# An expert's bias added by VectorE instead of by a product, and a residual sum moved from VectorE to GpSimd

## The chip, the core and the metric

The kernel runs on one core of one Trainium2 chip. Five engines work side by side, each through its own list of instructions in order: TensorE (PE, with its weight loads shown as PEld), VectorE (DVE), ScalarE (ACT), GpSimd (POOL) and SyncE (SP, which only issues transfers here). They meet through semaphores. The metric is the device time of one launch in microseconds (us). Before the change its median over three runs is 768.35 us (768.01 to 769.15).

## The reference

The input is 128 graphs of 128 nodes with 256 features. A graph layer comes first, then a layer of 16 experts with top-1 routing and a capacity of 1228 rows an expert.

```python
def gnn(X, A):                     # X: layer-normed x, A: adj, per graph
    Xw = X @ Wv + bv
    e = leaky_relu(sj[:, None, :] + si[:, :, None] + ab[0], 0.2)   # sj, si: Xw @ aw halves
    alpha = A * exp(e);  T = alpha / (alpha.sum(-1, keepdims=True) + 1e-12)
    H = 0;  Xk = X
    for k in range(3):
        H = H + Xk @ Wk[k] + bk[k];  Xk = T @ Xk
    return relu(H)

def experts(x):                    # x: all 16384 rows, layer-normed
    probs = softmax(x @ switch_w.T + switch_b);  route, p = argmax, max
    pos = rank of the row among those of its expert;  keep = pos < 1228
    y = x @ expert_w[route].T + expert_b[route]
    return where(keep, y, x) * p

x = x + gnn(layernorm(x), adj)
x = x + experts(layernorm(x))
```

## The kernel before

The graph layer goes graph by graph. One turn of the pipeline is called a slot here; slot `k` works on several graphs at once, each at another point of its way: graph `k` is multiplied with the weights, graph `k+2` is normalised by GpSimd (L475, `x`), and graph `k-2` (`LAG_X1`) gets its result. For that graph TensorE has summed the three products in PSUM (`ps_z0`), and VectorE adds the summed bias of the layer (L728, into `hb`), then does ReLU and the residual sum in one instruction (L739, `rows = max(hb, 0) + xin`). Mean and variance of the new row follow (L774, L798). TensorE transposes that row one slot later (L1188) for the logits (L1254); every fourth slot a group of four graphs is routed by some twenty small VectorE instructions. Ten slots behind its own (`LAG_OUT`) a graph's rows are scattered by GpSimd to a buffer in HBM, sorted by expert (L507, one indirect DMA for each graph).

From slot 32 on, as soon as enough rows of an expert are there, a slot also carries one tile of 128 rows of one expert. These 96 or so slots are called woven here; the tile is loaded by SP (L404), normalised by ScalarE (L646), transposed by TensorE (L1290), split in a rounded part (`xth`, ScalarE, L652) and a rest (`xtl`, VectorE, L1107, function `low`). TensorE then makes six products with the expert's weights and a seventh with its bias (L1311): `two_ones` (a matrix whose first two rows are ones) times `ebp` (the two parts of all 16 biases, in two partitions, all others zero). Which expert it is stands in a table (`tab_exp`), from which TensorE's sequencer loads a register (L1302). VectorE multiplies with the probability and adds the row (L1121, function `finish`), and GpSimd scatters the finished tile to the output (L524, a second indirect DMA in each woven slot). ScalarE also writes a default output for every graph (L588).

The tiles that are left when the graphs are through (46 of 143) run in a tail, `tile(i)` on each engine.

The order on each engine is written out by hand: `slot_fn(it, k)` of each engine's block lists what it does in a slot, `phase_a` calls it for all slots, and `woven(it, k)` and `tailed(it, k)` say which tile goes with it. GpSimd's list for a woven slot is: normalise (L475), scatter the tile (L524), scatter the row (L507), and in every fourth slot two powers and an update of the token numbers (L471, L485, L502). VectorE's list has `hb`, `finish`, `rows`, `xtl` of the next graph, the statistics, `svs` (a small operand that TensorE waits for, L783), `low`, and at the end the row softmax (`em`, `al`, `ri`, `tm`: L837, L846, L852, L857), whose `tm` TensorE transposes in the next slot (L1211).

## Time and profile before

| | |
|---|---|
| median of the runs | 768.35 us |
| the profiled execution | 767.28 us, its span 765.5 us |
| TensorE busy | 711.6 us (93%), granted clock 0.985 |
| VectorE busy | 647.9 us (85%) |
| ScalarE busy | 480.2 us (63%) |
| GpSimd busy | 444.1 us (58%) |

The span has four parts: a start up to about 26 us, 32 slots without a tile up to about 163 us, the woven slots up to about 664 us, and the last routing with the tail up to the end. A busy TensorE counts pipelined matmuls whose ends are modelled, so 100% does not by itself say that no faster pace is possible; it says that the engine was never seen waiting. Idle time of an engine that others do not wait for costs nothing.

### The profile page before, as it was taken

To read this page: it belongs to the slowest core of one execution; us is meant where nothing else is said; L and a number is where in the kernel's file an instruction comes from. 1 tells how busy PE (TensorE), PEld (TensorE's weight loads), DVE (VectorE), ACT (ScalarE), POOL (GpSimd) and SP (SyncE) were. 2 spreads that over 40 slices of the span, in tenths; PEclk is the share of its full clock that TensorE was granted. 3 is DMA by queue.
4 is the path that set the end of the run, shared out by engine and by line. 5 is a ranking of instruction groups with operands and counts; after the bars stand their busy time and mean duration, and the time that the engine had idled before them with its cause. 6 is when DMAs were issued, how large, how long until landed. Compare 5 with 4: busy or idle time off the path is not lost.

```text
span 765.5 us, 18802 instructions
## 1 busy us (share of the span) xinstructions
PE 711.6 (93%) x4791; PEld 624.2 (82%) x4791; DVE 647.9 (85%) x3100; ACT 480.2 (63%) x1504; POOL 444.1 (58%) x523
## 2 busy tenths in 40 slices
PE   1899999999999999999999999999999999877783
PEld 1788888778888888898889899898889899756663
DVE  3799999999989999899989999999989988785552
ACT  1457777766666666666666666666666766654551
POOL 4224445546666666666656666666666665575563
PEclk9999999999999999999999999999999999979998
DMA  9423444433344444444443344444443323353430
GB/s 266 118 85 97 138 138 154 151 127 119 123 144 153 147 146 153 128 150 139 146 141 118 121 143 149 145 140 147 134 134 128 115 89 101 99 167 112 120 104 1
DMA packets 93035, 100.15 MB, mean 131 GB/s; under 512 B 10427, under 2 KB 85240, under 8 KB 92930
## 3 DMA queue, kind: packets, MB, share of 16 engines
q1 hardware_dynamic: 77860, 66.74, 30.1%
q0 software_dynamic: 13008, 30.07, 10.8%
q10 hardware_dynamic: 2064, 2.13, 1.1%
q8 instruction: 44, 0.72, 0.4%
q14 instruction: 59, 0.48, 0.2%
HBM read 49.92 MB, written 54.72 MB: 137 GB/s over the span
## 4 chain that ended last, share of the span: by engine, by line
PE 86%; DVE 6%; issue 3%; ACT 1%; SPq 1%; DMA 1%; POOL 1%; POOLq 0%; DVEq 0%; ACTq 0%
PE ps_z12a L1160 11%; PE ps_z12b L1160 11%; PE ps_lgb L1160 9%; PE ps_z0a L1160 9%; PE ps_z0b L1160 8%; PE ps_lga L1254 6%; PE ps_z0b L1261 4%; PE ps_z0a L1261 4%; PE ps_z12b L1220 4%; PE ps_xt L1194 3%; PE ps_xt L1188 3%; PE ps_z12a L1220 3%; PE ps_lgb L1290 3%; PE ps_t L1242 2%; PE ps_t L1211 2%
## 5 line engine op out<-in xcount | busy, mean ns | idle before, releaser
L524 POOL DMA_INDIRECT out<-lent,tok x143 | 145.8, 1020 | 151.3 <-DVE lent L1121 136.0
L507 POOL DMA_INDIRECT rowbuf<-rows,idx x128 | 129.8, 1014 | 55.0 <-issue 30.1
L572 ACT CAST xth<-ps_xt 128x256 fp32r<-128x256 f32 x128 | 47.8, 373 | 123.6 <-PE ps_xt L1194 123.3
L475 POOL TENSOR_SCALAR x<-xin,nm,r 128x256 f32<-128x256 f32 x128 | 85.1, 665 | 27.6 <-PE ps_xt L1194 19.3
L1254 PEld LDWEIGHTS ps_lga<-swc,xft 128*128 128x128 f32 x512 | 76.8, 191 | 14.2 <-ACT xft L575 3.4
L646 ACT ACTIVATE x<-rin 128x256 f32<-128x256 f32 x143 | 86.8, 608 | 1.7 <-DMA rin<-rowbuf 1.7
L471 POOL TENSOR_TENSOR r<-ve,mhalf 128x4 f32<-128x4 f32 x32 | 34.2, 1069 | 77.7 <-ACT ve L618 77.7
L588 ACT ACTIVATE od<-rows,oc,oa 128x256 f32<-128x256 f32 x128 | 77.0, 602 | 0.1
L753 DVE TENSOR_TENSOR xtl<-ps_xt,xth 128x256 fp32r<-128x256 f32 x128 | 54.0, 422 | 20.6 <-ACT xft L575 19.6
L1254 PE MATMUL ps_lga<-swc,xft 128*128 128x16 f32 x512 | 66.2, 243 | 2.9 <-ACT xft L575 2.9
L1194 PE MATMUL ps_xt<-ident,x 128*128 128x128 f32 x256 | 49.5, 275 | 9.4 <-POOL x L475 8.5
L1160 PE MATMUL ps_z12b<-w12l,xth 128*128 128x512 f32 x128 | 57.7, 451 | 0.0
L1160 PE MATMUL ps_z12a<-w12l,xth 128*128 128x512 f32 x128 | 57.2, 447 | 0.0
L739 DVE SCALAR_TENSOR_TENSOR rows<-hb,xin 128x256 f32<-128x256 f32 x128 | 54.8, 429 | 1.5
L1160 PE MATMUL ps_lgb<-ewh,xth 128*128 x194 | 55.4, 367 | 0.5 <-issue 0.5
L817 DVE BATCH_NORM_STATS2 st<-xin 128x6 f32<-128x256 f32 x128 | 53.1, 415 | 1.5 <-DMA xin<-in_x 1.5
L1107 DVE TENSOR_TENSOR xtl<-ps_lgb,xth 128x256 fp32r<-128x256 f32 x112 | 46.8, 418 | 7.5 <-ACT xth L652 3.1
L774 DVE BATCH_NORM_STATS2 st<-rows 128x6 f32<-128x256 f32 x128 | 52.9, 413 | 0.0
L601 ACT ACTIVATE e<-ps_t,svs 128x128 f32<-128x128 f32 x128 | 47.1, 368 | 9.0 <-PE ps_t L1242 5.9
L652 ACT CAST xth<-ps_lgb 128x256 fp32r<-128x256 f32 x112 | 42.3, 378 | 15.6 <-PE ps_lgb L1290 15.5
L837 DVE TENSOR_TENSOR em<-e 128x128 f32<-128x128 f32 x128 | 38.3, 299 | 15.0 <-ACT e L602 12.0
L575 ACT COPY xft<-ps_xt 128x256 f32<-128x256 f32 x128 | 48.4, 378 | 3.8 <-PE ps_xt L1188 3.8
(205 smaller groups left out, 2358.8 us busy)
## 6 DMA issues: line engine op xcount, KB each, us to landing
rin<-rowbuf SPq DMA_DIRECT2D x143, 130.0 KB, 2.3
xin<-in_x SPq DMA_DIRECT2D x32, 512.0 KB, 4.0
out<-od SPq DMA_DIRECT2D x32, 512.0 KB, 5.4
ain<-in_adj SPq DMA_DIRECT2D x32, 256.0 KB, 4.6
ewr<-in_ewT SPq DMA_DIRECT2D x16, 256.0 KB, 2.9
out<-lent,tok POOLq DMA_INDIRECT x143, 3.0
rowbuf<-rin ACTq DMA_DIRECT2D x1, 2080.0 KB, 10.8
rowbuf<-rows,idx POOLq DMA_INDIRECT x128
```

The source lines that it names most:

```text
L475: pool.tensor_scalar(x0[:, g % 2, :], xin[:, g % BODY, :], nm1[:, q, g % G:g % G + 1], r1[:, q, g % G:g % G + 1], ALU.add, ALU.mult).then_ ...
L507: pool.indirect_dma_start(out=rowbuf, out_offset=bass.IndirectOffsetOnAxis(ap=idx[:, i:i + 1], axis=0), in_=rows[:, r, :], in_offset=None, ...
L524: pool.indirect_dma_start(out=out.rearrange("g n d -> (g n) d"), out_offset=bass.IndirectOffsetOnAxis(ap=tok[:, i % RY:i % RY + 1], axis=0 ...
L588: act.activation(od[:, b2 * G + j, :], rows[:, go % BODY, 0:D], ACT.Identity, bias=oc[:, b2, j:j + 1], scale=oa[:, b2, j:j + 1]).then_inc( ...
L646: act.activation(x0[:, xr(i), :], rin[:, i % RI, 0:D], ACT.Identity, bias=rin[:, i % RI, NMR:NMR + 1], scale=rin[:, i % RI, RSTD:RSTD + 1] ...
L739: dve.scalar_tensor_tensor(rows[:, r, 0:D], hb[:, g % 2, :], 0.0, xin[:, r, :], ALU.max, ALU.add).then_inc(s_x1, 1)
L753: dve.tensor_tensor(xtl[:, g % 2, :], ps_xt[:, 0:D], xth[:, g % 2, :].bitcast(F32), ALU.subtract).then_inc(s_x0l, 1)
L1160: return pe.matmul(psum_out, lhs_l if part == 2 else lhs_h, rhs_l if part == 1 else rhs_h, start=start, stop=stop, skip_group_check=True)
L1194: mm = pe.transpose(ps_xt[:, t * P:(t + 1) * P], x0[:, g % 2, t * P:(t + 1) * P], ident[:])
L1220: pe.matmul(ps_z12[d][:, D:2 * D], tt[:, d, :], z2[:, d, :], start=False, stop=True, skip_group_check=True).then_inc(s_tz2, 1)
L1254: mm = pe.matmul(ps_log[:, (b2 * G + j) * E:(b2 * G + j + 1) * E], xft[:, t * P:(t + 1) * P], swc[:, t, :], start=(t == 0), stop=(t == KT ...
L1261: pe.matmul(ps_z0[d][:, 0:D], tt[:, d, :], z1[:, d, :], start=False, stop=True, skip_group_check=True).then_inc(s_tz1, 1)
```

## The change

An expert's bias is no longer multiplied. All 16 biases (4096 numbers) are loaded once to every partition (`ebf`). In `low(i)`, right behind the rest part, VectorE adds bias times probability to the loaded row, in place; `finish(i)` is as before. VectorE therefore needs the expert's number as a register: it loads four at a time for the tiles of the woven slots and up to 16 at a time for the last 31. The product on TensorE, `two_ones`, the split of the biases and their way through HBM go.

The residual sum is rewritten: `relu(z + b) + x` is `max(z, -b) + (x + b)`. VectorE makes `hb = max(z, -b)` with `below = -b`; GpSimd makes `xb = x + b` ahead, and `rows = hb + xb`. Both additions stand in GpSimd's slot between the normalisation and the scatters. VectorE's statistics of the new row move from the middle of its slot to behind `low`.

```diff
@@ sync
-            sp.dma_start(ebr[:], eb).then_inc(d_eb, 16)
...
-            sp.wait_ge(s_eb, 2)
-            sp.dma_start(parts[0].bitcast(F32), ebh[:].bitcast(F32)).then_inc(d_ebp, 16)
-            sp.dma_start(parts[1].bitcast(F32), ebl[:].bitcast(F32)).then_inc(d_ebp, 16)
-            sp.wait_ge(d_ebp, 32)
-            sp.wait_ge(s_ebz, 1)
-            sp.dma_start(ebp[0:2, :].bitcast(F32), parts.rearrange("r e d -> r (e d)").bitcast(F32)).then_inc(d_ebp, 16)
+            sp.dma_start(ebf[:], eb.rearrange("(a e) d -> a (e d)", a=1).to_broadcast([P, E * D])).then_inc(d_eb, 16)
@@ gpsimd
-            pool.memset(two_ones[:].bitcast(F32), 0.0).then_inc(s_pc, 1)
...
+                g = k - LAG_X1
+                if valid(it, g):
+                    residual(it, g)
+                g = k - LAG_X1 + 1
+                if valid(it, g):
+                    biased_input(it, g)
                 i = woven(it, k - 1)
                 if i is not None:
                     scatter(i)
...
+            def biased_input(it, g):
...
+                ge(pool, s_x1, it * BODY + g - 1)
+                alone(pool)
+                pool.tensor_tensor(xb[:, g % 2, :], xin[:, g % BODY, :], bias[:], ALU.add).then_inc(s_xb, 1)
+
+            def residual(it, g):
...
+                pool.wait_ge(s_hb, it * BODY + g + 1)
+                pool.wait_ge(s_xb, it * BODY + g + 1)
+                alone(pool)
+                pool.tensor_tensor(rows[:, r, 0:D], hb[:, g % 2, :], xb[:, g % 2, :], ALU.add).then_inc(s_x1, 1)
...
-            pool.memset(ebp[:].bitcast(F32), 0.0).then_inc(s_ebz, 1)
@@ vector, slot_fn
-                    dve.tensor_tensor(hb[:, g % 2, :], ps_z0[g % 2][:, 0:D], bias[:], ALU.add).then_inc(s_hb, 1)
+                    dve.tensor_tensor(hb[:, g % 2, :], ps_z0[g % 2][:, 0:D], below[:], ALU.max).then_inc(s_hb, 1)
...
-                    dve.scalar_tensor_tensor(rows[:, r, 0:D], hb[:, g % 2, :], 0.0, xin[:, r, :], ALU.max,
-                                             ALU.add).then_inc(s_x1, 1)
...
-                    dve.bn_stats(st2[:, g % 2, :], rows[:, g % BODY, 0:D]).then_inc(s_st2, 1)
...
+                g = k - LAG_X1
+                if valid(it, g):
+                    dve.wait_ge(s_x1, n(g))
+                    dve.bn_stats(st2[:, g % 2, :], rows[:, g % BODY, 0:D]).then_inc(s_st2, 1)
@@ vector, tiles
+            def experts_of(i):
...
+                if i < STEPPED and i % G == 0 or i >= STEPPED and (i - STEPPED) % LOADED == 0:
+                    dve.wait_ge(s_tab, step_of(i))
+                    m = G if i < STEPPED else min(LOADED, NT - i)
+                    _, at_i = nc.values_load_multi_w_load_instructions(
+                        tab_exp[0:1, i:i + m], [mybir.EngineType.DVE], min_val=0, max_val=E - 1)
...
             def low(i):
...
+                experts_of(i)
+                own = rin[:, i % RI, :]
+                dve.scalar_tensor_tensor(own[:, 0:D], ebf[:, bass.ds(at.pop(i) * D, D)], own[:, PROB:PROB + 1],
+                                         own[:, 0:D], ALU.mult, ALU.add).then_inc(b_row, 1)
@@ tensor
-                pe.matmul(y, two_ones[:], ebp[:, bass.ds(e * D, D)], start=False, stop=True,
-                          skip_group_check=True).then_inc(b_y, 1)
+                mm.then_inc(b_y, 1)
```

The first place where the order moves is GpSimd's list in the woven slots. These rows of before cover one slot with the powers of the fourth slot and the one behind it; `x` is the normalised graph, `out<-lent` the scatter of a tile, `rowbuf<-rows` that of a row.

```order
L471 TENSOR_TENSOR r<-ve,mhalf 128x4 [waits s_ve1]
L475 TENSOR_SCALAR x<-xin,nm,r 128x256 [waits s_r1,s_x0t]
L524 DMA out<-lent,tok 16384x256 [waits b_fin]
L485 TENSOR_TENSOR rows<-ve,mhalf 128x4 [waits s_ve2]
L502 TENSOR_SCALAR rows<-rows 128x4 [waits s_slot,s_tok]
L507 DMA rowbuf<-rows,idx 21696x260 [waits s_tok]
L475 TENSOR_SCALAR x<-xin,nm,r 128x256 [waits s_x0t]
L524 DMA out<-lent,tok 16384x256 [waits b_fin]
```

The same place in the changed kernel:

```order
L461 TENSOR_TENSOR r<-ve,mhalf 128x4 [waits s_ve1]
L465 TENSOR_SCALAR x<-xin,nm,r 128x256 [waits s_r1,s_x0t]
L527 TENSOR_TENSOR rows<-hb,xb 128x256 [waits s_xb,s_hb,d_scat2,s_odw]
L517 TENSOR_TENSOR xb<-xin,bias 128x256 [waits s_x1]
L537 DMA out<-lent,tok 16384x256 [waits b_fin]
L481 TENSOR_TENSOR rows<-ve,mhalf 128x4 [waits s_ve2]
L498 TENSOR_SCALAR rows<-rows 128x4 [waits s_slot,s_tok]
L503 DMA rowbuf<-rows,idx 21696x260 [waits s_tok]
L465 TENSOR_SCALAR x<-xin,nm,r 128x256 [waits s_x0t]
L527 TENSOR_TENSOR rows<-hb,xb 128x256 [waits s_hb,s_xb]
```

Two additions of 128x256 stand between the normalisation and the first scatter in every slot, and the first of them waits for VectorE's `hb`.

The second place is the second half of VectorE's list in a woven slot, from `low` to the `tm` that TensorE waits for. Before:

```order
L817 BN_STATS st<-xin 128x6
L1107 TENSOR_TENSOR xtl<-ps_lgb,xth 128x256 [waits b_hi]
L837 TENSOR_TENSOR em<-e 128x128 [waits s_e]
L937 TENSOR_TENSOR pos<-ps_t,pos 128x80 [waits s_pos,s_pre]
L846 ISA al,rs<-ain,em 128x128 [waits d_a3,s_em]
L846 ISA rs 128x1
L946 TENSOR_TENSOR sel<-oh,pos 128x64 [waits s_oh,s_pos]
L852 RECIPROCAL ri<-rs 128x1 [waits s_al]
L950 TENSOR_REDUCE slot<-sel 128x4 [waits s_ro]
L857 TENSOR_SCALAR tm<-al,ri 128x128 [waits s_ri]
```

After, in the fourth slot, in which the expert numbers are loaded:

```order
L805 BN_STATS st<-xin 128x6
L1118 TENSOR_TENSOR xtl<-ps_lgb,xth 128x256 [waits b_hi]
L1110 TENSOR_LOAD tab_exp [waits s_tab]
L1110 ISA x8
L1122 ISA
L1122 SCALAR_TENSOR_TENSOR rin<-ebf,rin 128x256
L820 BN_STATS st<-rows 128x6 [waits s_x1]
L829 TENSOR_TENSOR em<-e 128x128 [waits s_e]
L934 TENSOR_TENSOR pos<-ps_t,pos 128x80 [waits s_pos,s_pre]
L838 ISA al,rs<-ain,em 128x128 [waits d_a3,s_em]
L838 ISA rs 128x1
L943 TENSOR_TENSOR sel<-oh,pos 128x64 [waits s_oh,s_pos]
```

A load of four registers, the bias addition and the statistics of the new row (which wait for GpSimd's `rows`) now stand ahead of `em`, `al` and `tm`.

## Rows read from the trace of the kernel before

**Rows 1.** The page: busy time by engine, and the chain that ended last
```profile
PE 711.6 (93%) x4791; PEld 624.2 (82%) x4791; DVE 647.9 (85%) x3100; ACT 480.2 (63%) x1504; POOL 444.1 (58%) x523
...
PE 86%; DVE 6%; issue 3%; ACT 1%; SPq 1%; DMA 1%; POOL 1%; POOLq 0%; DVEq 0%; ACTq 0%
```

**Rows 2.** Busy us (x instructions), PE, PEld, DVE, ACT, POOL, in two stretches
```profile
200.00:600.00 400.00, 400.00 (x2784) 359.07 (x2783) 362.76 (x1823) 269.87 (x864) 255.95 (x288) 1.00 0.44 139
70.00:160.00 90.00, 88.40 (x563) 73.22 (x562) 84.66 (x408) 64.19 (x213) 45.46 (x57) 1.00 0.44 139
```

**Rows 3.** Line 728 (one `hb` a slot), 200:600: ns min/median/max, first and last start
```profile
L728 DVE TENSOR_TENSOR hb<-ps_z0a,bias x39: 415/418/421, 201.5 to 597.7; 128x256 f32<-128x256 f32 x39
```

**Rows 4.** The same line in 70:160, slots without a tile
```profile
L728 DVE TENSOR_TENSOR hb<-ps_z0b,bias x10: 408/415/422, 77.0 to 155.1; 128x256 f32<-128x256 f32 x10
```

**Rows 5.** GpSimd's lines in 200:600: busy us, mean ns, then idle before
```profile
L524 POOL DMA_INDIRECT out<-lent,tok x77 | 79.8, 1037 | 90.6 <-DVE lent L1121 78.7 <-issue 11.9
L507 POOL DMA_INDIRECT rowbuf<-rows,idx x77 | 77.4, 1005 | 33.5 <-issue 17.7 <-POOL rows L502 15.0 <-PE ps_xt L1194 0.8
L475 POOL TENSOR_SCALAR x<-xin,nm,r 128x256 f32<-128x256 f32 x77 | 53.9, 701 | 6.9 <-POOL r L471 2.7 <-PE ps_xt L1194 1.9
...
L502 POOL TENSOR_SCALAR rows<-rows 128x4 f32<-128x4 f32 x19 | 5.3, 281 | 0.0
```

**Rows 6.** Line 475 in 40:62 (before any scatter) and in 200:600
```profile
L475 POOL TENSOR_SCALAR x<-xin,nm,r x4: 557/558/691, 48.0 to 55.7; 128x256 f32<-128x256 f32 x4
```
```profile
L475 POOL TENSOR_SCALAR x<-xin,nm,r x77: 558/730/856, 200.6 to 596.8; 128x256 f32<-128x256 f32 x77
```

**Rows 7.** GpSimd in order of time, 408 to 413: start, length, [idle before]
```profile
408.61 1.03 POOL L524 DMA_INDIRECT out<-lent,tok  x1 [0.17 <-issue]
409.95 0.97 POOL L507 DMA_INDIRECT rowbuf<-rows,idx  x1 [0.30 <-issue]
410.95 0.86 POOL L475 TENSOR_SCALAR x<-xin,nm,r 128x256 f32<-128x256 f32 x1
```

**Rows 8.** PE and DVE in order of time, 408 to 412
```profile
410.08 0.29 DVE L857 TENSOR_SCALAR tm<-al,ri 128x128 f32<-128x128 f32 x1
...
410.27 0.28 PE L1311 MATMUL ps_lgb<-ebp,two_ones 128*128 x1
...
410.39 0.38 PE L1188 MATMUL ps_xt<-ident,rows 128*128 128x128 f32 x2
...
411.29 0.14 PEld L1211 LDWEIGHTS ps_t<-ident,tm 128*128 128x128 f32 x1
```

**Rows 9.** VectorE's residual and statistics of the row in 200:600
```profile
L739 DVE SCALAR_TENSOR_TENSOR rows<-hb,xin x77: 412/416/436, 202.4 to 598.5; 128x256 f32<-128x256 f32 x77
```
```profile
L774 DVE BATCH_NORM_STATS2 st<-rows x77: 395/419/423, 203.6 to 599.7; 128x6 f32<-128x256 f32 x77
```

**Rows 10.** TensorE's sequencer loads an expert number (L1302), whole run
```profile
L1302 PEldq TENSOR_LOAD <-tab_exp x143: 295/306/859, 163.5 to 753.7; - x143
L1302 PEldq FUSED_REGOPS  x143: 151/151/165, 164.0 to 754.0; - x143
L1302 PEldq SEQ_ASSERT  x143: 18/18/24, 164.3 to 754.2; - x143
```

**Rows 11.** Waits in 70:160: us in total, times, longest
```profile
PEld ps_t L1242 <- DVE svs L783: 4.6, 13, 1.0
```

**Rows 12.** VectorE in the tail, in order of time
```profile
716.62 0.16 DVE L1119 TENSOR_TENSOR tok<-rin,mask 128x1 uint32<-128x1 f32 x1 [0.71 <-PE ps_z0a L1311]
...
718.12 0.16 DVE L1119 TENSOR_TENSOR tok<-rin,mask 128x1 uint32<-128x1 f32 x1 [0.46 <-PE ps_z0b L1311]
...
719.88 0.16 DVE L1119 TENSOR_TENSOR tok<-rin,mask 128x1 uint32<-128x1 f32 x1 [0.72 <-PE ps_z0a L1311]
```

**Rows 13.** The chain that ended last, in order of time, two of VectorE's links
```profile
684.24 0.69 DVE lent_w L1089
684.95 0.69 DVE lent_b L1091
```

**Rows 14.** GpSimd in order of time, at the start
```profile
4.29 3.51 POOL L548 MEMSET ebp<- 128x4096 f32 x1
16.37 2.01 POOL L471 TENSOR_TENSOR r<-ve,mhalf 128x4 f32<-128x4 f32 x1 [8.57 <-ACT ve L618]
```

More of the change, by code:

```diff
@@ L35 @@
 LAG_TILE = 16
+LOADED = 16
 REST = 2
@@ L64, in graph_then_experts @@
     rowbuf = nc.dram_tensor("rowbuf", [ROWS, ROW], F32, kind="Internal").ap()
-    parts = nc.dram_tensor("parts", [2, E, D], F32R, kind="Internal").ap()
     with ExitStack() as ctx:
@@ L116, in graph_then_experts @@
         bias = sb("bias", [P, D])
+        below = sb("below", [P, D])
         hb = sb("hb", [P, 2, D])
-        ebr = sb("ebr", [E, D])
-        ebh = sb("ebh", [E, D], F32R)
-        ebl = sb("ebl", [E, D], F32R)
-        ebp = sb("ebp", [P, E * D], F32R)
+        xb = sb("xb", [P, 2, D])
+        ebf = sb("ebf", [P, E * D])
         ewr = sb("ewr", [P, EPP, KT, D])
@@ L208, in graph_then_experts @@
         d_eb = sem("d_eb")
[L209 to L211 removed]
+        s_below = sem("s_below")
+        s_xb = sem("s_xb")
+        b_row = sem("b_row")
         d_ew = [sem(f"d_ew{q}") for q in range(EPP)]
@@ L448, in _ @@
             pool.memset(w0r[:, :, D:W0C], 0.0).then_inc(s_pc, 1)
-            pool.memset(two_ones[:].bitcast(F32), 0.0).then_inc(s_pc, 1)
-            pool.wait_ge(s_pc, 7)
-            pool.memset(two_ones[0:2, :].bitcast(F32), 1.0).then_inc(s_pc, 1)
+            pool.wait_ge(s_pc, 6)
             pool.affine_select(ident[:], onesf[:], pattern=[[1, P]], compare_op=ALU.is_equal, fill=0.0,
@@ L679, in set_up @@
                 link(dve.tensor_tensor(bias[:], bias[:], bkr[:, 2, :], ALU.add))
+                dve.tensor_scalar(below[:], bias[:], -1.0, None, ALU.mult).then_inc(s_below, 1)
                 dve.wait_ge(s_wh, 1)
@@ L693, in set_up @@
                 link(dve.tensor_scalar(cvec[:, 2:3], cvec[:, 1:2], SLOPE, None, ALU.mult))
-            def expert_biases(it, k):
-                if isinstance(it, int) and it == 0 and k == 0:
-                    dve.wait_ge(d_eb, 16)
-                    dve.tensor_copy(ebh[:], ebr[:]).then_inc(s_eb, 1)
-                if isinstance(it, int) and it == 0 and k == 1:
-                    dve.wait_ge(s_eb, 1)
-                    dve.tensor_tensor(ebl[:], ebr[:], ebh[:].bitcast(F32), ALU.subtract).then_inc(s_eb, 1)
             def slot_fn(it, k):
@@ L849, in slot_fn @@
                     own_positions(it, gp)
+                g = k - LAG_X1
+                if valid(it, g):
+                    dve.wait_ge(s_st2, n(g))
+                    alone(dve)
+                    dve.bn_aggr(mv2[:, g % (2 * G), :], st2[:, g % 2, :]).then_inc(s_mv2, 1)
+                g = k
                 if valid(it, g):
@@ L1102, in last_tiles @@
                                   ALU.bitwise_and).then_inc(s_tab, 1)
+            at = {}
+            def experts_of(i):
+                if i == 0:
+                    dve.wait_ge(d_eb, 16)
+                if i < STEPPED and i % G == 0 or i >= STEPPED and (i - STEPPED) % LOADED == 0:
[3 more added lines that the diff above has]
+                        tab_exp[0:1, i:i + m], [mybir.EngineType.DVE], min_val=0, max_val=E - 1)
+                    for j in range(m):
+                        at[i + j] = at_i[j]
             def low(i):
@@ L1308, in expert @@
                     w = bass.ds(e * EW + t * D, D)
-                    product(y, part, xth[:, c, ts], xtl[:, c, ts], ewh_f[:, w], ewl_f[:, w],
-                            start=(part == 0 and t == 0))
-                pe.matmul(y, two_ones[:], ebp[:, bass.ds(e * D, D)], start=False, stop=True,
-                          skip_group_check=True).then_inc(b_y, 1)
+                    mm = product(y, part, xth[:, c, ts], xtl[:, c, ts], ewh_f[:, w], ewl_f[:, w],
+                                 start=(part == 0 and t == 0), stop=(part, t) == PARTS[-1])
+                mm.then_inc(b_y, 1)
             def tile(i):
```

34 lines of the change are left out of this document (11 added, 23 removed).

## The prediction, on record before the changed kernel ran

> **What bounds the kernel now.** I read the page first. TensorE is busy 93% of the span and holds 86% of the chain that ended last; VectorE follows with 85%, GpSimd has 58% [rows 1]. Shares over the whole span mix stages, so I cut the span. In the 400 us from 200 to 600, all woven slots, TensorE is busy for all 400, VectorE for 363, GpSimd for 256 [rows 2]. The pace there is read from one instruction that comes once in two slots: 39 `hb` out of one PSUM buffer, first at 201.5, last at 597.7, so 76 slots in 396.2 us, 5.21 us a slot [rows 3]. In the slots without a tile it is ten in 78.1 us, 18 slots, 4.34 us each [rows 4]. TensorE sets both paces. The question is what another engine needs for one slot after the change; whoever needs more than TensorE sets the pace of 96 woven slots, and 0.1 us a slot is 9.6 us in all.
>
> **TensorE, what goes.** The bias product shows 282 ns, but matmuls overlap: it starts at 410.27 and the next one at 410.39, so it holds the engine for 0.12 us [rows 8]. Without it TensorE needs 5.09 us for a woven slot. Were nothing else slower, that would be 96 x 0.12 = 11.5 us.
>
> **GpSimd, what comes.** Its own work for one woven slot before the change: 255.95 us busy in 77 slots is 3.32 us [rows 2, 5]. To it belong gaps in which it can do nothing else: 0.17 us ahead of a scatter that follows an arithmetic instruction and 0.30 ahead of one that follows another scatter [rows 7], 0.47 a slot; in every fourth slot the scatter behind the token update starts 0.83 us late (15.0 us over 18 cases [rows 5]) instead of 0.30, 0.13 a slot; and 0.24 us ahead of an `x` that waits for its power (2.7 us over 11 cases [rows 5]), 0.06 a slot. Together 4.0 us. It fits in 5.21 because it idles: 78.7 us waiting for VectorE's finished tile [rows 5].
>
> The change adds two additions of 128x256 with both inputs in SBUF, which the trace does not show on this engine. Nearest is the normalisation of the same shape with one tensor input: 558 ns when little else runs, and a median of 730 ns in the woven slots, 172 ns more with the same work [rows 6]. The same kind of instruction on 128x4 takes 281 ns [rows 5], so of the 558 some 280 are for the 252 further columns. An addition has a second tensor to read. If that is free and nothing slows it, it takes 0.56 us; if it doubles the part that goes with the columns, 0.84, and with the 0.17 of the woven slots 1.01. These are the two ends. I take 0.80: the nearest row is the 0.73 of the same stage, and I add a quarter of the possible second reading. Then GpSimd needs 4.0 + 2 x 0.80 = 5.60 us a slot, 0.39 more than the 5.21 of now. It has no idle time left, so the cover that it had is gone and the slot becomes 5.60: 96 x 0.39 = +37.4 us. At the ends the slot is 5.12 (GpSimd no longer the bound) or 6.02 (96 x 0.81 = +78 us).
>
> The Trainium skill, GPSIMD Engine Reference, section 3.1, gives about 2.6 cycles an element for a two-input `tensor_tensor` and 4497 ns at 2048 columns, because both inputs share one read port. By that a 256-column addition would be an estimated 0.56 us and some fixed part, and with the page's rate the slot would be an estimated 5.1 to 5.7 us. No row here shows this operation, so the sum above does not use it.
>
> The new wait: `rows` on GpSimd waits for `hb` of the same slot, and behind it in GpSimd's list stand `xb`, both scatters and the next `x`. VectorE's statistics wait for `rows`, and behind them `em`, `al` and `tm`, for which TensorE waits. As GpSimd comes to `rows` late rather than early at 5.6 us a slot, `hb` is there already, and I add nothing for this wait. TensorE takes the row only a slot later.
>
> **VectorE.** The residual instruction goes, 0.416 us [rows 9]; the bias addition has the same shape and both inputs in SBUF too, so I take 0.42. In sum nothing, but the place differs: the residual stood ahead of `svs`, the addition stands ahead of `tm`, and the row statistics, 0.419 us [rows 9], go there too. So 0.84 us more stand between `low` and `tm`. Before, `tm` ended at 410.37 and TensorE loaded it at 411.29, 0.92 us to spare [rows 8]. That covers it, just. In every fourth slot a register load comes on top: 0.31 us for the load and four times 0.15 + 0.02 [rows 10], 0.99 us, with nothing queued on VectorE meanwhile but `low`. In that slot `tm` is up to 0.9 late. Against 5.09 us a slot this would cost 0 to 0.9 us in four slots; against 5.60 it hides behind GpSimd, since TensorE then waits 0.5 us a slot anyway. Cost nothing, with GpSimd as the cover.
>
> **Slots without a tile.** GpSimd needs 4.0 - 1.04 - 0.30 = 2.66 us and 1.60 for the additions, 4.26, under the 4.34 of now: hidden, just. VectorE loses 0.42 us a slot, and TensorE's wait for `svs`, 4.6 us in 20 slots [rows 11], should go; only 1.6 of those 90 us were lost to TensorE's matmuls [rows 2]. I take -1.5 us for 32 slots.
>
> **Start.** The memset of `ebp`, 3.51 us, ends at 7.8 and GpSimd waits for ScalarE until 16.37 [rows 14]: nothing. The 2 MB load of `ebf` is first used in slot 32: nothing. The new `below` is one unlinked VectorE instruction, under 0.4 us.
>
> **Tail and last routing.** In the tail two tiles take 3.26 us, 716.62 to 719.88, alternating 1.50 and 1.76: a loop over two tiles, product, `finish`, register load, next product in the same PSUM buffer [rows 12]. One bias product drops out of each loop: 23 x 0.12 = -2.8 us. VectorE waits 0.46 to 0.72 us a tile there [rows 12], which covers the 0.42 of the addition. Its register loads are not covered all: three of four values in the last routing, where VectorE is the chain [rows 13], 3 x 0.99 = +3.0; two of 16 and 15 values, 0.31 + 16 x 0.17 = 3.0 and 2.9, less the 1.6 us by which `low` is ahead, +2.7; and some five additions in that chain, +2. Together about +4.8.
>
> **The sum.** Made against the profiled execution, 767.28 us: +37.4 - 1.5 + 4.8 = +40.7, so 808.0. The median of the runs is 1.07 us above it: 809 us.
>
> **The rivals.**
> Rival 1, the additions are cheap and VectorE's order decides. If an addition takes 0.60 us or less, GpSimd needs at most 5.2 and TensorE's 5.09 would show. Then the fourth slot with its register load costs 0 to 0.9 us, against 4 x 0.12 = 0.48 gained in those four slots: 24 groups give -11.5 to +10 us, the middle near nothing, and with the +3.3 of the other stages 766 to 779, about 771. For it: the unhindered 558 ns. Against it: the 730 ns in the very stage.
>
> Rival 2, faster. The product's 0.12 us come out in full because VectorE's and GpSimd's work hides: 768.35 - 11.5 - 2.8 - 1.5 = 752.6, up to 764 if the register loads cost their part. It decides from an addition of under 0.54 us, as 4.0 + 2 x 0.54 = 5.08. Against it speaks that this is below the shortest one-input instruction of the same shape in the stage, 558 ns [rows 6]. For it speaks only that the profile calls its own spans on GpSimd rough.
>
> Rival 3, the two engines hold each other. The x instruction grew by 0.17 us where VectorE is busy 91% of the time [rows 2, 6], so GpSimd's reading collides with VectorE's. If each of three instructions now meets such a hold, and VectorE's `em`, `al` and the new addition are held as well, additions of 1.1 us and more give a slot of 6.2 and 768.35 + 96 x 0.99 + 3.3 = 867; from 1.01 us on, over 849. For it: the growth is there. Against it: `rows` on GpSimd falls beside `finish` and `xtl` on VectorE, which read PSUM.
> The Trainium skill, SBUF — State Buffer, "Who interferes with whom", says so as a rule: a VectorE instruction with two SBUF inputs and a GpSimd instruction that reads SBUF exclude each other for a whole instruction. The trace agrees in direction (558 and 730 ns); full exclusion would have stretched `rows` on VectorE, whose maximum is 436 against a median of 416 ns.
>
> **Chances.** The forecast, GpSimd sets the pace with additions of 0.60 to 1.0 us: 0.68, by itself 771 to 848. Rival 1: 0.13. Rival 2: 0.10. Rival 3: 0.09. The range of 770 to 846 leaves out rival 2 and rival 3, 0.19. A difference under 0.2% (1.5 us) cannot be told from none. Faster: rival 2 and a fifth of rival 1, 0.13. Same: a quarter of rival 1, 0.03. Slower: the rest, 0.84.
>
> **What would show it.** In the woven stretch of the changed kernel GpSimd is busy over 90% of the time and its waits for VectorE's finished tile are gone; TensorE idles some 0.5 us a slot; the two additions show 0.7 to 0.9 us each; VectorE's row statistics wait for GpSimd's `rows`. `hb` comes every 5.5 to 5.7 us. The prediction is wrong if GpSimd still idles there; if the additions show under 0.6 us; or if TensorE waits for `tm` while GpSimd waits for `hb`, which would make VectorE's order the cause. If the pace stays 5.2 and the time is up, the tail would be where I mis-sized.

## The result and the profile after

The changed kernel takes 878.16 us, median of four runs (876.62 to 879.85), against 768.43 of the kernel before on the same chip: a ratio of 1.143, 95% interval 1.140 to 1.145. It is slower, as forecast, but by 110 us and not by 41, and outside the range. The profiled execution has a span of 876.6 us.

The page of the changed kernel, busy time and chain, to be held against [rows 1]:

```profile
span 876.6 us, 19360 instructions
...
PE 748.4 (85%) x4648; PEld 610.6 (70%) x4648; DVE 749.5 (86%) x3114; ACT 479.0 (55%) x1504; POOL 613.0 (70%) x776
...
DVE 55%; issue 17%; PE 13%; ACT 6%; DVEq 4%; POOL 2%; SPq 1%; DMA 1%; POOLq 0%; ACTq 0%
```

TensorE held most of the chain before; now VectorE holds 55% and GpSimd 2%. The same two windows as [rows 2], busy us of PE, PEld, DVE, ACT, POOL, and the `hb` instruction as in [rows 3, 4] (count, ns min/median/max, first and last start):

```profile
70.00:160.00 90.00, 82.41 (x498) 65.25 (x498) 79.20 (x334) 55.50 (x185) 67.82 (x88) 1.00 0.37 114
200.00:600.00 400.00, 365.46 (x2337) 299.28 (x2336) 367.47 (x1573) 232.02 (x743) 304.16 (x380) 1.00 0.37 119
```
```profile
L734 DVE TENSOR_TENSOR hb<-ps_z0b,below x10: 416/417/421, 69.9 to 159.1; 128x256 f32<-128x256 f32 x10
...
L734 DVE TENSOR_TENSOR hb<-ps_z0a,below x33: 410/417/421, 202.5 to 589.9; 128x256 f32<-128x256 f32 x33
```

A woven slot now takes (589.9 - 202.5)/64 = 6.05 us where it took 5.21, and a slot without a tile (159.1 - 69.9)/18 = 4.96 where it took 4.34. In 96 woven slots the first is 96 x 0.84 = 81 us. Cut at the first tile's scatter and at the last `hb`, the execution is 17.9 us longer before the woven slots, 81.2 in them and 12.0 after them. The three make up the 111.1 us between the two spans.

No engine is full. GpSimd is busy 76% of the woven window, TensorE 91%, VectorE 92%. The next two views say who waits. First GpSimd's lines in 200:600 (busy us, mean ns, then idle before and what ended it), as in [rows 5]:

```profile
L527 POOL TENSOR_TENSOR rows<-hb,xb 128x256 f32<-128x256 f32 x66 | 48.3, 732 | 37.2 <-DVE hb L734 37.2
L517 POOL TENSOR_TENSOR xb<-xin,bias 128x256 f32<-128x256 f32 x66 | 48.0, 727 | 0.0
L465 POOL TENSOR_SCALAR x<-xin,nm,r 128x256 f32<-128x256 f32 x66 | 38.3, 581 | 5.8 <-POOL r L461 3.9
```

Then the waits of 200:600 (us in total, times, longest):

```profile
POOL rows L527 <- DVE hb L734: 37.2, 33, 1.9
PEld ps_t L1258 <- DVE svs L776: 27.3, 32, 1.5
PEld ps_t L1227 <- DVE tm L855: 24.9, 49, 1.4
DVE rin L1122 <- issue: 20.4, 17, 1.5
```

GpSimd waits for VectorE's `hb`, TensorE waits for VectorE's `svs` and `tm`, and VectorE stands still 20 us ahead of its bias addition, waiting for nothing that the profile shows as a wait. The additions are as short as hoped, 0.73 us. What became long is found among VectorE's smallest instructions, in 200:600 of the kernel after:

```profile
L895 DVE TENSOR_TENSOR lg<-lg,swb 128x64 f32<-128x64 f32 x16 | 23.6, 1477 | 0.0
...
L1010 DVE TENSOR_TENSOR_SCAN upto<-ones_e,full 128x17 f32<-128x17 f32 x16 | 11.1, 691 | 0.0
L956 DVE TENSOR_TENSOR rows<-nm,rows 128x4 f32<-128x4 f32 x17 | 10.2, 602 | 0.0
L1014 DVE TENSOR_TENSOR start<-done,upto 128x16 f32<-128x16 f32 x16 | 10.2, 635 | 0.0
L1047 DVE SCALAR_TENSOR_TENSOR want<-start,done 128x16 f32<-128x16 f32 x17 | 8.8, 518 | 0.0
L1055 DVE TENSOR_TENSOR done<-want,have 128x16 f32<-128x16 f32 x17 | 7.5, 440 | 0.0
```

The same work in the kernel before:

```profile
L898 DVE TENSOR_TENSOR lg<-lg,swb 128x64 f32<-128x64 f32 x19 | 4.2, 219 | 0.0
...
L1013 DVE TENSOR_TENSOR_SCAN upto<-ones_e,full 128x17 f32<-128x17 f32 x19 | 3.7, 195 | 0.0
L1017 DVE TENSOR_TENSOR start<-done,upto 128x16 f32<-128x16 f32 x19 | 3.0, 159 | 0.0
```

Six instructions grew from 0.16 to 0.22 us each to between 0.44 and 1.48, some 3.3 us in four slots. All six read two tensors in SBUF. Their neighbour in the list that reads PSUM (the `lg` that comes first, L889, 215 ns) is unchanged. One place of the kernel after in order of time, VectorE, GpSimd, then TensorE (start, length, [idle before]):

```profile
221.47 1.56 DVE L895 TENSOR_TENSOR lg<-lg,swb 128x64 f32<-128x64 f32 x1
223.07 0.22 DVE L900 TENSOR_REDUCE mx<-lg 128x4 f32<-128x64 f32 x1
223.20 0.15 DVE L776 TENSOR_TENSOR svs<-ps_z0b,cvec 128x4 f32<-128x4 f32 x1
```
```profile
221.70 0.56 POOL L465 TENSOR_SCALAR x<-xin,nm,r 128x256 f32<-128x256 f32 x1
222.23 0.71 POOL L527 TENSOR_TENSOR rows<-hb,xb 128x256 f32<-128x256 f32 x1
222.91 0.71 POOL L517 TENSOR_TENSOR xb<-xin,bias 128x256 f32<-128x256 f32 x1
```
```profile
223.41 0.32 PE L1258 MATMUL ps_t<-ident,svs 128*128 128x128 f32 x1 [1.14 <-DVE svs L776]
```

`lg` starts 0.23 us ahead of GpSimd's `x` and ends at 223.03, just behind the end of the first addition (222.94). `svs` stands behind it in VectorE's list, and TensorE loses 1.14 us. Which of GpSimd's three instructions it waited for cannot be read from their places here, since GpSimd's spans are rough. The runs below show it: in all but one or two of their slots `lg` starts 0.23 us ahead of `x`, as here, and there it takes 0.21 us where no addition follows (e10), 0.86 to 0.87 where one does (e6, e7) and 1.56 where two do. Each addition costs it 0.65 to 0.70 us, `x` nothing.

### The profile page after: what moved, and what is told of

Read it like the earlier page. It is cut to its first block, busy times and chain, and to the rows that moved or that the text cites. A ratio compares the mean times of both kernels' runs of the same rounds, so it can differ in the third digit from the quotient of the medians.

```text
span 876.6 us, 19360 instructions
## 1 busy us (share of the span) xinstructions
PE 748.4 (85%) x4648; PEld 610.6 (70%) x4648; DVE 749.5 (86%) x3114; ACT 479.0 (55%) x1504; POOL 613.0 (70%) x776
## 4 chain that ended last, share of the span: by engine, by line
DVE 55%; issue 17%; PE 13%; ACT 6%; DVEq 4%; POOL 2%; SPq 1%; DMA 1%; POOLq 0%; ACTq 0%
DVE st L820 4%; DVE xtl L1118 4%; DVE lg L895 4%; DVE rin L1122 4%; DVEq L1110 4%; DVE st L805 4%; DVE em L829 3%; PE ps_z0a L1176 3%; DVE xtl L750 3%; PE ps_z0b L1176 2%; ACT x L658 2%; DVE lent L1137 2%; DVE hb L734 2%; DVE start L1014 2%; DVE al L838 2%
## 5 line engine op out<-in xcount | busy, mean ns | idle before, releaser
L527 POOL TENSOR_TENSOR rows<-hb,xb 128x256 f32<-128x256 f32 x128 | 94.8, 741 | 77.4 <-DVE hb L734 76.4
L1122 DVE SCALAR_TENSOR_TENSOR rin<-ebf,rin 128x256 f32<-128x256 f32 x143 | 69.3, 484 | 44.3 <-issue 44.3
L517 POOL TENSOR_TENSOR xb<-xin,bias 128x256 f32<-128x256 f32 x128 | 93.2, 728 | 0.0
L465 POOL TENSOR_SCALAR x<-xin,nm,r 128x256 f32<-128x256 f32 x128 | 76.1, 595 | 12.8 <-POOL r L461 7.7
L1176 PE MATMUL ps_lgb<-ewh,xth 128*128 x194 | 53.1, 355 | 12.9 <-DVE xtl L1118 10.5
L1258 PE MATMUL ps_t<-ident,svs 128*128 128x128 f32 x128 | 37.3, 291 | 27.4 <-DVE svs L776 26.2
L591 ACT COPY tt<-ps_t 128x128 f32<-128x128 f32 x128 | 34.4, 269 | 42.5 <-PE ps_t L1227 41.9
L1227 PE MATMUL ps_t<-ident,tm 128*128 128x128 f32 x128 | 38.2, 298 | 20.7 <-DVE tm L855 19.9
```

What stands on the lines that cost most here:

```text
L465: pool.tensor_scalar(x0[:, g % 2, :], xin[:, g % BODY, :], nm1[:, q, g % G:g % G + 1], r1[:, q, g % G:g % G + 1], ALU.add, ALU.mult).then_ ...
L517: pool.tensor_tensor(xb[:, g % 2, :], xin[:, g % BODY, :], bias[:], ALU.add).then_inc(s_xb, 1)
L527: pool.tensor_tensor(rows[:, r, 0:D], hb[:, g % 2, :], xb[:, g % 2, :], ALU.add).then_inc(s_x1, 1)
L1122: dve.scalar_tensor_tensor(own[:, 0:D], ebf[:, bass.ds(at.pop(i) * D, D)], own[:, PROB:PROB + 1], own[:, 0:D], ALU.mult, ALU.add).then_inc ...
L1176: return pe.matmul(psum_out, lhs_l if part == 2 else lhs_h, rhs_l if part == 1 else rhs_h, start=start, stop=stop, skip_group_check=True)
```

## The experiments

All ratios are to the kernel before on the same chip, and the edits are abbreviated and stand against the changed kernel. "Hold" below means what the last timeline shows: a VectorE instruction that shows no end while a GpSimd instruction runs.

**The two halves of the change, each alone.** `e1_residual_only` keeps the bias product on TensorE; `e2_bias_only` keeps residual and statistics where they were.

```
e1:  - dve.scalar_tensor_tensor(own, ebf[e], prob, own)    + pe.matmul(y, two_ones, ebp[e])
e2:  - pool.tensor_tensor(rows, hb, xb, add)   + dve.scalar_tensor_tensor(rows, hb, 0.0, xin, max, add)
```


> The residual half of the change alone: the bias is multiplied by TensorE as before, VectorE makes max(z, -b) and GpSimd both additions, with the statistics of the row behind the tile's rest part. Theory A (GpSimd's two adjacent additions hold up VectorE's instructions that read two tensors from SBUF; lg<-lg,swb went from 219 to 1477 ns, upto 195 to 691, start 144 to 635, rows 161 to 602, want 165 to 518, done 165 to 440, together 3.3 us in four slots): these long times are still there, VectorE's own work is 0.42 + 0.30 us a slot less than in the changed kernel, and the kernel is clearly slower than before, about 800 to 845 us. Theory B (VectorE's order and the register load are the cause, the holds fall beside waits): near before, 765 to 780 us. Theory C, my forecast (GpSimd sets the pace by its own work): GpSimd over 90% busy in the woven slots.

> The bias half of the change alone: VectorE adds bias times probability and loads the expert numbers, no bias product on TensorE; the residual sum stays on VectorE as before, GpSimd adds nothing. Theory A: the small instructions are at 0.15 to 0.22 us again; VectorE has 0.42 us more a slot and a stall of 1.2 us in every fourth, 0.72 a slot against some 0.45 us of idle time before, so 96 x 0.2 to 0.4 us more: 785 to 810 us. Theory B: as slow as the changed kernel without its 0.42 us saved elsewhere, 850 us and more.

Measured: e1 822.61 us (1.072, 1.069 to 1.075), e2 802.05 us (1.046, 1.043 to 1.049). Both halves cost, 56 and 35 us, 91 of the 110; some 19 us come only when they meet. In e1 `lg` takes 1487 ns in the mean, in e2 214: the long instructions belong to the additions on GpSimd. In e2, where GpSimd does nothing new, VectorE still stands still 21.1 us ahead of the bias addition. That is a second cause.

**Is it the reading of SBUF?** `e3_quiet_gpsimd` has a memset of 128x800 in the place of each addition, `e4_loud_gpsimd` an addition into a scratch buffer; in both VectorE makes the row in its `hb` instruction.

```
- pool.tensor_tensor(rows[...], hb[...], xb[...], ALU.add)
+ pool.memset(idle[:, 0, :], 0.0)                                   # e3, 128x800
+ pool.tensor_tensor(idle[:, 0, 0:D], xin[...], bias[:], ALU.add)   # e4
```


> The changed kernel with GpSimd's two additions replaced by two memsets of 128x800 into scratch, about as long (0.73 us each) and with the same waits and signals, which read nothing from SBUF. VectorE makes max(z, 0) + xin in the one instruction that made hb; the graph layer's summed bias is left out. Theory A: VectorE's small instructions fall to 0.15 to 0.22 us, 0.86 us a slot is given back: 790 to 805 us. Theory C (GpSimd's time itself): as the changed kernel, 870 us or more.

> The same as the kernel with the two memsets on GpSimd, VectorE included, but with two additions of 128x256 on GpSimd (xin + bias, both into scratch) in their place; the graph layer's summed bias is left out of the result. The only difference between the two is that GpSimd reads two tensors from SBUF. Theory A: the holds are back, 865 to 890 us. Theories B and C: the same time as with the memsets, within 1%.

Measured: e3 847.1 us (1.106, 1.100 to 1.111), e4 876.68 us (1.143, 1.139 to 1.147). e4 is the changed kernel once more, whatever the additions read. e3 did not do what it was made for. `lg` is back at 219 ns, so a memset does not hold it, but other instructions are long. VectorE and GpSimd in e3, in order of time:

```profile
402.41 1.73 DVE L1046 TENSOR_SCALAR tab_exp<-tab_row 128x4 uint32<-128x4 uint32 x1
402.62 0.78 POOL L526 MEMSET idle<- 128x800 f32 x1
402.64 1.50 DVE L930 RECIPROCAL rows<-sx 128x4 f32<-128x4 f32 x1
402.76 1.38 DVE L780 TENSOR_TENSOR svs<-ps_z0a,cvec 128x4 f32<-128x4 f32 x1
...
403.33 0.78 POOL L516 MEMSET idle<- 128x800 f32 x1
```

`tab_exp`, with one SBUF input, ends at 404.14, when the second memset (403.33 + 0.78) does, and the reciprocal and `svs` behind it end with it. The run left the question open.

**The hold by itself.** `e9_hold_alone` is no form of this kernel: ten measurements, each with 24 linked VectorE instructions (small ones, but for two measurements) beside ten GpSimd instructions or none.

> A small kernel that computes nothing of the reference: on VectorE 24 chained instructions at a time, beside ten instructions on GpSimd. VectorE line 62 is an addition of 128x16 with both inputs in SBUF and GpSimd idle; 66 the same beside GpSimd additions of 128x256; 71 with one input in PSUM; 76 a one-input tensor_scalar; 81 a reduction; 86 the two-input addition beside memsets of 128x800; 91 beside a one-input tensor_scalar of 128x256; 96 and 101 an addition of 128x256 beside GpSimd additions and alone; 106 the one-input form beside memsets. Theory A (GpSimd's reading keeps VectorE from reading a second tensor out of SBUF): 66 holds until GpSimd's additions end, 0.6 us and more each or the whole run of ten; 71, 81 and 86 as 62, about 0.15 us; 91 held too. If the hold were general, 71 and 81 would be as long as 66. If there were none, 66 would be as 62 and the long times of the changed kernel have another cause.

Measured, by line of VectorE (ns min/median/max): L62 alone, L66 beside 128x256 additions, L71 the same with one input in PSUM, L76 with one input, L81 a reduction; L86 beside memsets of 128x800, L91 beside GpSimd's one-input instruction of 128x256, L106 one input beside memsets.

```profile
L62 DVE TENSOR_TENSOR c<-a,b x24: 174/174/176, 5.1 to 10.0; 128x16 f32<-128x16 f32 x24
...
L66 DVE TENSOR_TENSOR c<-a,b x24: 174/176/647, 10.4 to 19.8; 128x16 f32<-128x16 f32 x24
...
L71 DVE TENSOR_TENSOR c<-ps,b x24: 173/174/175, 20.3 to 25.1; 128x16 f32<-128x16 f32 x24
...
L76 DVE TENSOR_SCALAR c<-a x24: 174/175/646, 27.3 to 36.8; 128x16 f32<-128x16 f32 x24
...
L81 DVE TENSOR_REDUCE c<-a x24: 169/170/171, 37.2 to 41.9; 128x1 f32<-128x16 f32 x24
...
L86 DVE TENSOR_TENSOR c<-a,b x24: 174/175/177, 44.2 to 49.0; 128x16 f32<-128x16 f32 x24
...
L91 DVE TENSOR_TENSOR c<-a,b x24: 174/176/337, 51.6 to 58.0; 128x16 f32<-128x16 f32 x24
...
L106 DVE TENSOR_SCALAR c<-a x24: 174/176/762, 85.0 to 95.0; 128x16 f32<-128x16 f32 x24
```

With a mean of 369 ns in L66, (369 - 175) x 24 / (647 - 175) gives ten held instructions of 24, one for each addition. An instruction with two SBUF inputs, or with the one of a tensor_scalar, is held by an addition for up to the addition's own length; an input in PSUM, or a reduction, never. A memset holds the instruction with one SBUF input and not the one with two, which is what e3 had run into. GpSimd's one-input instruction (408 ns) holds too, but for less. GpSimd's additions took 723 ns there. They grew to 912 only beside VectorE additions of 128x256, which grew from 425 to 593 in the mean: there both sides lose.

**How much by each addition, and where they stand.** `e6_one_sum` makes one addition on GpSimd (the graph layer's bias is left out). `e7_sums_apart` makes both, but with a scatter between them.

```
e6:  - pool.tensor_tensor(xb, xin, bias, add)     rows = hb + xin
e7:  residual(it, g); scatter(i); biased_input(it, g)      # was: residual, biased_input, scatter
```


> The changed kernel with one addition on GpSimd instead of two: VectorE makes max(z, 0), GpSimd adds xin; the graph layer's summed bias is left out. Theory A: VectorE's held instructions lose half of their hold or more (the longest, 1.5 us, was behind two additions in a row, now 0.8), 825 to 845 us. Theory C: GpSimd's work falls by 0.73 us a slot, and the kernel by as much.

> The changed kernel, complete, with GpSimd's second addition (xb) moved behind the tile's scatter, so that the two additions are 1 us apart. Theory A: no instruction is held over both, lg falls from 1.5 us to 0.8 at most, but xb now holds others: 850 to 875 us. Theory C: the same time as the changed kernel, since GpSimd does the same work.

Measured: e6 834.77 us (1.089), e7 895.0 us (1.168), the last above its theory's 850 to 875. One addition fewer gives back some 42 us. Parting the two shortens `lg` (822 ns) and hits others: `oc` takes 718 ns (175 in the kernel after), `idx` 632 (128), `rise` 565 (151), the bias addition 555 (490). A place without instructions that can be held is not found by moving one addition; this was a miss.

**The register loads.** `e5_no_register_load` is the changed kernel with expert 0's bias for every tile, so VectorE loads no number. `e8_stats_back` puts the row's statistics back ahead of `svs`.

```
e5:  - nc.values_load_multi_w_load_instructions(tab_exp[0:1, i:i + m], [DVE])     ebf[:, 0:D]
e8:  bn_stats(st2, rows), bn_aggr(mv2, st2): from behind low and al to behind dropped and default_factors
```


> The changed kernel without VectorE's register loads: the bias of expert 0 is added to every row (the other 15 are left out). Everything else, the addition on VectorE included, stays. Theory A: the loads stall VectorE 1.2 us in every fourth slot and VectorE is the bound, so 24 x 1.2 = 29 us plus 5 to 8 in the tail go: 835 to 850 us. If the loads hide behind GpSimd's hold: no more than 10 us.

> The changed kernel with the statistics of the finished row (L774 and L783 of before) back at their old places in VectorE's slot, ahead of svs; everything else as after, the result is the same. Theory (VectorE's small instructions held by GpSimd's additions, and the register loads, make the difference of 110 us): the place of the statistics matters little; 865 to 900 us, and lg and upto stay above 600 ns in the mean. Rival (the order of VectorE's list is at fault, since 0.84 us stand between low and tm): tm is 0.42 us earlier in each slot, so the woven slots give back up to 96 x 0.42 = 40 us: 835 to 850 us.

Measured: e5 838.6 us (1.093, 1.092 to 1.095), e8 864.28 us (1.129, 1.122 to 1.137), just under the 865 to 900 of its theory. The loads cost some 38 us by the ratios, though the prediction had hidden all those of the woven slots. The order of VectorE's list is worth some 10 us (4 to 16 over the interval of e8) and not 40. In the kernel after, the load and what it leaves of VectorE:

```profile
L1110 DVEq FUSED_REGOPS  x143: 183/183/212, 178.7 to 841.1; - x143
L1110 DVEq SEQ_ASSERT  x143: 23/23/35, 179.0 to 841.3; - x143
L1110 DVEq TENSOR_LOAD <-tab_exp x30: 339/342/1559, 178.1 to 835.7; - x30
```
```profile
400.46 0.51 DVE L1122 SCALAR_TENSOR_TENSOR rin<-ebf,rin 128x256 f32<-128x256 f32 x1 [1.20 <-issue]
```

0.34 + 4 x 0.21 = 1.18 us, and VectorE is empty for 1.20.

**Taking the causes out one by one.** `e10_no_sums` leaves GpSimd only the signals (the graph layer's bias is left out, VectorE makes the row in its `hb` instruction); `e11_no_sums_no_load` takes the register loads away as well; `e14_short_ops` puts three tensor_scalar of 128x4 in the place of each addition, a list nearly as long that reads little.

```
e10: - pool.tensor_tensor(rows, hb, xb, add)   + pool.sem_inc(s_x1, 1)
e14: + for j in range(3): pool.tensor_scalar(idle[:, h, 4*j:4*j+4], onesf[:, 0:4], 1.0, None, mult)
```


> After, with GpSimd only handing the signals on: neither addition is made there, VectorE makes the row in its hb instruction (the graph's bias is left out of the sum), so GpSimd executes what it executed before the change. The expert's bias by VectorE and the register loads stay. Theory (holds by GpSimd's two additions): all small VectorE instructions are back at 150 to 250 ns, lg under 300 ns in the mean; against after the time falls by 60 to 80 us, to 795 to 815 us; what is left over before is the register loads and the 0.42 us of bias addition. Rival (the waits between the two engines cost, not the holds): signals and order are unchanged, so the time stays above 845 us though lg is short.

> As e10_no_sums, and VectorE takes the bias of expert 0 for every tile, so that it loads no register. Theory: the register loads stop VectorE for 1.2 us in every fourth slot and in the tail, worth 30 to 40 us here as beside the additions (39.6 us): 760 to 775 us, where TensorE's 0.12 us a tile without the product begins to show. Rival (the load cost 39.6 us only because VectorE was held and late anyway): under 15 us against e10_no_sums, 785 to 800 us.

> As e10_no_sums, but GpSimd makes three tensor_scalar instructions on 128x4 in the place of each addition (about 0.28 us each, 0.84 us together, where an addition takes 0.73): its list is as long as after, but it reads SBUF for few columns. Theory (an addition costs by holding VectorE's instructions while it reads): VectorE's small instructions stay under 350 ns in the mean and the time stays near e10_no_sums, 801 to 820 us. Rival (GpSimd's longer list and its lateness cost, not the holds): as after, 860 to 890 us.

Measured: e10 801.12 us (1.043, 1.041 to 1.045), e11 762.74 us (0.992, 0.991 to 0.994), e14 826.28 us (1.075, 1.073 to 1.077). VectorE's `tm`, `df` and `lg` in e14, 200:600, and GpSimd's stand-ins:

```profile
L864 DVE TENSOR_SCALAR tm<-al,ri 128x128 f32<-128x128 f32 x71 | 25.5, 360 | 1.9
...
L913 DVE TENSOR_TENSOR df<-lg,mx 128x64 f32<-128x64 f32 x18 | 9.8, 542 | 0.0
...
L904 DVE TENSOR_TENSOR lg<-lg,swb 128x64 f32<-128x64 f32 x18 | 3.9, 218 | 0.0
```
```profile
L513 POOL TENSOR_SCALAR idle<-onesf 128x4 f32<-128x4 f32 x432 | 89.6, 230 | 12.2 <-DVE rows L742 12.2
```

The six stand-ins of a slot keep GpSimd busy for 89.6/72 = 1.24 us, the two additions for (48.3 + 48.0)/66 = 1.46. Both theories of e14 are half right: the six long instructions of after are short again (`lg` 218 ns, the scan 196), yet the time is not that of e10. And e14 is not free of holds. `df` takes 542 ns (279 in e10), `al` 366 (288), `tm` 360 (291) and `tab_exp` 341 (158), together some 18 us in these 400, and each long one stands beside one of GpSimd's scatters. TensorE waits for `tm` there.

The steps, as ratios: e11 0.992; with the register loads (e10) +0.050; with the stand-ins on GpSimd (e14) +0.032; with additions that read SBUF, as after, +0.068. In us of the kernel before: -6, +39, +25, +52. The fourth also holds 0.22 us more of GpSimd's time a slot. The third was not parted: it is GpSimd's longer list, or the holds that come with its later scatters, or both. So the holds are worth some 52 us, less what the 0.22 costs, and up to 77 if the third step is theirs too.

One more comparison: e2, where VectorE keeps the residual and GpSimd gets nothing, takes 1.046, and e10, where VectorE has 0.42 us a slot less to do, 1.043. The place of the statistics differs between the two, so this is no clean test. But no run shows that the work taken from VectorE was worth anything, even where GpSimd did not have to do it.

**Is there a form that gains?** `e12_preset` leaves VectorE and GpSimd alone in the woven slots: ScalarE writes the bias into the PSUM buffer ahead of the products. `e13_bias_rows` and `e15_grouped_numbers` let VectorE add the bias, with no additions on GpSimd, from a ring that SyncE fills; in the last, SyncE loads its numbers for 31 tiles of the tail in fours.

```
e12: + act.copy(ps_tile[:, D:2*D], ebf[:, expert])          products start with start=False
e13: + sp.dma_start(ebt[:, i % RI, :], eb[expert].to_broadcast([P, D]))     dve: own += ebt[:, i % RI, :] * prob
e15: + nc.values_load_multi_w_load_instructions(tab_row[0:1, i:i + 4], [SP]), and tab_exp
```


> The kernel before with the bias product taken out in another way: for the 97 woven tiles ScalarE copies the expert's bias into the PSUM buffer between the row of one tile and the turn of the next, and TensorE's products accumulate on it; ScalarE loads the four expert numbers, VectorE and GpSimd do what they did before. In the tail VectorE adds the bias to the row as after. Theory (TensorE set the pace of before, and the loss of the change lies in what VectorE and GpSimd were given): TensorE's slot falls by up to 0.12 us, 96 x 0.12 = 11.5 less up to 5 us for the tail: 757 to 768 us. Rival (the chain row of one tile, preset, turn of the next, high, low, product has no slack, or ScalarE's register load of 1.2 us stops TensorE in every fourth slot): 775 to 800 us.

> No bias product and no additions on GpSimd; the residual is VectorE's again, as before. VectorE adds the expert's bias to the row as after, but no engine that computes loads a register for it: SyncE, which loads a number for every tile already, loads the expert's number too and brings that expert's bias by one more transfer a tile (1 KB from DRAM to each of 128 partitions) into a ring of eight buffers. The result is the same as before. Theory (the change lost its time by the additions and by the register loads, and VectorE's 0.42 us for the bias addition itself fits): 760 to 768 us. Rival (VectorE's list, 0.42 us longer and with the addition ahead of tm, is what stops TensorE, as in e2_bias_only, where the residual also stayed on VectorE): 780 to 800 us. Second rival: 128 KB more a tile delay the gathers of the tiles: TensorE waits for x of the tile, 775 us and more.

> As e13_bias_rows, but for the 31 tiles of the last routing SyncE loads its register values four tiles at a time and not one by one. The result is the same as before. In e13_bias_rows the woven part ended when that of before did (last hb at 662.7 against 663.4), and the 26 us that it lost came after it, where SyncE needs 2.2 to 2.4 us a tile (1.1 us from one transfer's issue to the next, two a tile) and ScalarE waited 27.3 us for the rows. Theory (SyncE's loads by single values set the pace of that tail): the tail gives back 31 x 0.6 = 19 us or so: 770 to 778 us. Rival (the further 128 KB a tile are themselves late there): 788 to 795 us, as e13_bias_rows.

Measured: e12 773.92 us (1.007, 1.005 to 1.008), e13 793.13 us (1.032, 1.031 to 1.034), e15 785.63 us (1.022, 1.020 to 1.025). All three are slower than their theories had them. e12 leaves the woven tiles without the right bias, for a reason that was not found, so only its time is read: its `hb` comes every (590.1 - 201.3)/76 = 5.12 us,

```profile
L750 DVE TENSOR_TENSOR hb<-ps_z0a,bias x39: 414/417/425, 201.3 to 590.1; 128x256 f32<-128x256 f32 x39
```

against 5.21 before. So the product is worth 0.10 us a woven slot once nobody else gets slower. Its last `hb` is 8.6 us earlier than before; the tail, with VectorE's addition and register loads, is 16.4 us longer. In e13 the last `hb` starts at 662.7, before at 663.4: VectorE's addition (0.54 us there) costs the woven slots nothing that the lost product does not pay. It loses 27 us behind them, where ScalarE waits for the tile. e13's rows (page) and SyncE in order of time:

```profile
L654 ACT ACTIVATE x<-rin 128x256 f32<-128x256 f32 x143 | 86.3, 605 | 28.9 <-DMA rin<-rowbuf 27.3
```
```profile
727.18 0.33 SPq L396 DMA_DIRECT2D rin<-rowbuf  x1
728.33 0.29 SPq L398 DMA_DIRECT2D ebt<-in_eb  x1
729.40 0.33 SPq L396 DMA_DIRECT2D rin<-rowbuf  x1
```

2.2 us a tile are more than the tail's 1.63 [rows 12]. Loading in fours gave back 8 us of the 19 expected; ScalarE still waits 19.9 us for its rows, and what holds the rest (15 tiles ahead of the last routing, or the transfers themselves) was not parted. Of all the forms only e11 was faster than the kernel before, and it leaves work out.

## Why the prediction was wrong

- **TensorE's product, right.** 0.12 us a tile was read off two starts; e12 shows 0.10 a woven slot. e11 as a whole gains 6 us where the sum for TensorE alone was 14; what takes the other 8 is not shown.
- **GpSimd's additions, right in size, wrong as the pace.** 0.80 us was taken, 0.73 measured. By the prediction's own working that makes GpSimd need 4.0 + 1.46 = 5.46 us a slot, and 5.46 it did not set: it is busy 304.16/66 = 4.61 us of 6.05 and waits 37.2 us for `hb`. So the sum's main term, +37.4 us, named a loss that did not happen that way. Its longer list is not free, though: e14 against e10, 25 us, part of it in holds beside the scatters.
- **The step that failed: "Cost nothing, with GpSimd as the cover".** It spoke for VectorE. It is wrong twice. First, VectorE's small instructions were priced as before, 0.16 to 0.22 us; beside GpSimd's additions they show up to 1.56 us, and what stands behind them (`svs`, `tm`) is what TensorE waits for. The steps from e10 over e14 to after put 52 of 110 us on this, and up to 77. Second, the register load of 0.99 us in every fourth slot was hidden behind a GpSimd pace of 5.60 us that never came. It measured 1.2 us on the engine that now ends the chain: e11 against e10, 38 us, of which 25.9 come before the last row of a graph (start 682.9 against 657.0) and 12 behind it.
- **Rival 3 had the mechanism and was argued down from the wrong engine.** It got 0.09 because `rows` on VectorE never took more than 436 ns. But the other engine can be the one that waits, and in the kernel before it was GpSimd. Of the 77 `x` in 200:600, the 18 with no VectorE instruction of two SBUF inputs beside them took 0.56 to 0.58 us, and the 21 with a whole `rows` (L739) beside them 0.79 to 0.86, such as the 0.86 of [rows 7]. That one's neighbour, and an `x` with its neighbour that reads PSUM:

```profile
411.07 0.41 DVE L739 SCALAR_TENSOR_TENSOR rows<-hb,xin 128x256 f32<-128x256 f32 x1
...
434.52 0.56 POOL L475 TENSOR_SCALAR x<-xin,nm,r 128x256 f32<-128x256 f32 x1
...
434.71 0.40 DVE L1107 TENSOR_TENSOR xtl<-ps_lgb,xth 128x256 fp32r<-128x256 f32 x1
```

  So the exclusion stood in the rows before the change. In size the rival was wrong too: the additions did not stretch to 1.1 us but took 0.73, and it was VectorE's small instructions that waited. The Trainium skill, SBUF — State Buffer, "Who interferes with whom", says that a VectorE instruction with two SBUF inputs contends with a GpSimd instruction that reads SBUF and not with one that only writes it; the trace agrees (up to 647 ns beside additions, 177 beside memsets, 174 alone). It also names `tensor_scalar`, with one input, among those that can contend, and says that `tensor_reduce` never does; the trace agrees (646 and 171).
- **Smaller slips.** The bias addition was priced at 0.42 us and took 0.49 in the woven slots. Rival 1's range of 766 to 779 us does not follow from its own terms: -11.5 to +10 us in the woven slots and +3.3 elsewhere give 760 to 782. And the sign "TensorE waits for `tm` while GpSimd waits for `hb`" came (24.9 and 37.2 us), but it did not mean that VectorE's order was the cause: e8 puts some 10 us on the order.
- **The wait of `rows` for `hb`, wrong.** Nothing was added for it, as GpSimd was to come late. GpSimd comes early and waits 37.2 us in 33 of 66 slots.
- **Slots without a tile, wrong in sign.** -1.5 us was taken, +17.9 came. `hb` comes there every 4.96 us after, 4.92 in e1 (70.0 to 158.5), 4.36 in e2 (77.2 to 155.7). So it is the additions again; GpSimd's 4.26 us, "hidden, just", was never what decided.
- **Tail and last routing, too small.** +4.8 was taken, +12.0 came. e10's rest behind the last row is 115.9 us and e11's 103.8 (before 102.1): it is the register loads, 12 us and not the 5.7 of the prediction.

## What to carry to other kernels

Before work goes to GpSimd, list VectorE's instructions that take their inputs from SBUF alone and that another engine waits behind; the shortest are the dearest, since each may last as long as one or two GpSimd instructions, however little it has to do. A trace in which VectorE is never late does not clear the pair: look at the same time whether GpSimd's instructions stretch. A register load on an engine is idle time of that engine: count it as busy unless the engine is seen to wait at that very place. And when a change hides one engine behind another, price the first engine anew under the second one's traffic before the cover is used.
